# A low-rank layer's norm begun in the attention before it, its gates in two unequal parts, and its outputs in six PSUM banks

## The chip, the cores and the metric

The kernel runs on one core of a Trainium2 chip. The time is device microseconds of one launch, median of 3 runs. One profiled execution goes with it; all rows come from that one.

## What is computed

Eight layers are applied in turn to `x`, 16 batches of 128 rows of 128 numbers, all float32. The change touches the last two: a causal cross-attention with 16 heads, and a low-rank layer with softmax gates. Cut to them, the reference is:

```python
x = x + _L3_xattn_ref(_layernorm(x, axis=-1), ctx_1024, ctx_1024, ...)
x = x + _L3_ffn_ref(_layernorm(x, axis=-1), weight, gate_w, lora_U, lora_V)
return x

def _L3_ffn_ref(x, weight, gate_w, lora_U, lora_V):
    scaling = 1.0 / lora_U.shape[1]                       # 1/16
    xt = x.reshape(-1, D_in)
    gate = jax.nn.softmax(xt @ gate_w.T, axis=-1)         # 8 gates a row
    base = xt @ weight.T
    t = jnp.einsum('nh,erh->ner', xt, lora_U)             # 8 x 16 low-rank numbers
    lora = jnp.einsum('ne,eor,ner->no', gate, lora_V, t)
    return (base + scaling * lora).reshape(B, S, -1)
```

## The kernel before, in words

**Order.** `build` calls eight layer functions one after the other. Each opens a `Block` in which every engine has its own program; engines meet only at semaphores, and all of them at the barrier between two blocks. The sequence in each engine's program is written out by hand. `x` stays in SBUF as 16 batches of 128x128, and `xnT` is the normalised and transposed copy that the matmuls read.

**The attention** (`cross_attention`, tag `l3`, `causal=True`, keys made ahead). Every engine runs a software pipeline over `b` from 0 to B + 4 = 20. In iteration `b`, TensorE makes scores of batch `b` for the row maxima and of batch `b - 2` for the exponentials, weighs the values of batch `b - 3` (`weigh`, L503), turns the result (`turn`, L511), transposes it back (`flip_back`, L531) and multiplies by the output weight for batch `b - 4` (`project_out`, L536). ScalarE makes exponentials (L609) and moves results (L614, L618). GpSimd zeroes what lies past the diagonal (L430), once for each half of a batch; `weigh` waits for both halves. VectorE takes maxima, normalises (L688, L690), adds to `x` (L696), and takes the row statistics of batch `b - 5` (L126, L129). From `b` = 16 on there are no more maxima: the pipeline drains. Three PSUM banks form a ring (`Banks`) whose users take turns in a fixed order. After its 32 diagonal steps GpSimd computes the reciprocal standard deviation of batches 0 to 11 by a power (`scale_known`; L134, L137). TensorE ends with 12 transposes of the identity that nothing reads (L222), and the barrier follows.

**The low-rank layer** (`gated_lora`, tag `l3f`). It has three stretches.

- The norm (`RowNorm`). GpSimd makes the last four reciprocals, VectorE normalises 13 batches (L186) and ScalarE 3 (L200), TensorE transposes each (L195) into two banks `turn_ps`, and ScalarE copies four at a time to `xnT` (L211).
- The projections and gates. TensorE projects each batch to 128 low-rank numbers and 8 logits (L2256), into `both_ps`, which has six banks of three batches each; two unused slots repeat the last batch. VectorE takes maxima of the logits and subtracts (L2335, L2337), ScalarE makes exponentials (L2309), VectorE sums, inverts and forms the gates (L2342 to L2344). This is done in two halves of nine slots, `HALF = CHUNKS // 2 = 3` banks each.
- The chunks. There are six chunks `k`, of three batches, the last of one. VectorE multiplies the low-rank numbers by the gates (`lower`, L2349), TensorE transposes the product into the same bank of `both_ps` (`flip`, L2272), ScalarE copies it out (L2313), and TensorE adds two matmuls in one bank of `turn_ps`, `base` (L2267) and `widen` (L2278). VectorE adds that bank to `x` (`add`, L2355), and SyncE stores the chunk (L2248). Since there are two such banks, `base(k + 1)` waits for `add(k - 1)`: `pe.wait_ge(added, k - 1)` in `base`.

Of the kernel before, what the change touches and what calls it, by code (L numbers as in the profile page):

```python
# [15 lines left out]
P = 128  # L16
# [278 lines left out]
def cross_attention(nc, m, w, tag, meanwhile, masked_keys=False, causal=False, arrived=None, load_x=None, keys=None):  # L295
# [4 lines left out]
    with cleared_semaphores(nc, m) as new_semaphore, ExitStack() as ctx:  # L300
# [97 lines left out]
        def _(pool):  # L398
# [26 lines left out]
            if causal:  # L425
                for c in range(B):
                    for half in range(2):
# [3 lines left out]
                                                channel_multiplier=-1).then_inc(past_kept, 1)  # L431
            row_stats.scale_known(pool)

        @block.tensor
        def _(pe):
# [78 lines left out]
            def flip_late(i):  # L514
# [38 lines left out]
            for b in range(B + 5):  # L553
# [28 lines left out]
        def _(act):  # L582
# [55 lines left out]
            for b in range(B + 5):  # L638
# [14 lines left out]
                if exists(b - 2):  # L653
                    exponentials(b - 2, 1)
                if arrived is not None and b in LATE_GROUPS:
                    store_late_flips(LATE_GROUPS[b])
# [4 lines left out]
        def _(dve):  # L661
# [44 lines left out]
            for b in range(B + 5):  # L706
# [21 lines left out]
                if exists(b - 5):  # L728
                    dve.wait_ge(added, b - 4)
                    row_stats.take(dve, b - 5, b - 4)  # L730


# [1471 lines left out]
def gated_lora(nc, m, w, tag, meanwhile):  # L2204
# [3 lines left out]
    CHUNKS, BOTH = -(-B // PER), P + E  # L2208
    HALF = CHUNKS // 2
    x, xnT, identity = m["x"], m["xnT"], m["identity"]  # L2210
    with cleared_semaphores(nc, m) as new_semaphore, ExitStack() as ctx:  # L2211
# [3 lines left out]
        def ps(name, shape):  # L2215
# [12 lines left out]
            [new_semaphore(f"{tag}_{n}") for n in ("low_made", "flipped", "flip_stored", "out_made", "added", "stored")]  # L2228
        norm = RowNorm(nc, m, new_semaphore, tag, sb("xn", [P, B, D]), [turn_ps[i % 2][:, :, :] for i in range(NCH)],
                       sb("away", [P, B]))  # L2230
        block = ctx.enter_context(nc.Block())

        def batches(k):
            return range(PER * k, min(PER * k + PER, B))

        def held(t, k):
# [3 lines left out]
        def _(pool):  # L2240
            norm.pool(pool)

# [9 lines left out]
        def _(pe):  # L2252
            mm = nc.tensor.matmul

            def project(slot):
                ins = mm(both[:, slot // PER, slot % PER, :], xnT[:, min(slot, B - 1), :], w["down_gate"][:, :],  # L2256
                         start=True, stop=True)
                if slot + 1 in (HALF * PER, CHUNKS * PER):
                    ins.then_inc(both_made, 1)

            def base(k):
                if k < 2:
                    norm.wait_stored(pe, NCH - 2 + k)
                else:
                    pe.wait_ge(added, k - 1)
                for q, b in enumerate(batches(k)):
                    mm(turn_ps[k % 2][:, q, :], xnT[:, b, :], w["weight"][:, :], start=(q == 0), stop=False)  # L2267

# [6 lines left out]
            def widen(k):  # L2275
                pe.wait_ge(flip_stored, k + 1)
                for q, b in enumerate(batches(k)):
                    ins = mm(turn_ps[k % 2][:, q, :], low_t[:, b, :], w["up"][:, :], start=False,  # L2278
                             stop=(b == batches(k)[-1]))
# [12 lines left out]
            base(0)  # L2292
            base(1)
            flip(0)
            for k in range(CHUNKS):
                if k + 1 < CHUNKS:
                    flip(k + 1)
                    if k:
                        base(k + 1)
                widen(k)  # L2300

        @block.scalar
        def _(act):
            for i in range(NCH):
                norm.act(act, i)
            for h in range(2):
                part = slice(h * HALF * PER, (h + 1) * HALF * PER)
                act.wait_ge(below_made, h + 1)
                nc.scalar.activation(exps[:, part, :], below[:, part, :], ACT.Exp).then_inc(exps_made, 1)  # L2309
# [7 lines left out]
        def _(dve):  # L2317
            V = nc.vector
            chain = Chain(dve, step, 0)

            def part(h):
                return slice(h * HALF * PER, (h + 1) * HALF * PER)

            def logits(h):
                return both[:, h * HALF:(h + 1) * HALF, :, P:BOTH]

# [3 lines left out]
            def each_gate(row, h):  # L2330
                return row[:, part(h)].unsqueeze(2).broadcast_to([P, HALF * PER, E])

# [20 lines left out]
            def add(k):  # L2353
                dve.wait_ge(out_made, k + 1)
                V.tensor_tensor(held(x, k), held(x, k), turn_ps[k % 2][:, 0:len(batches(k)), :], ALU.add).then_inc(added, 1)  # L2355
# [8 lines left out]
            share(1)  # L2364
# [1076 lines left out]
```

## Time and profile before

| what | us |
|---|---|
| median of 3 runs | 1135.13 |
| lowest and highest of them | 1132.43, 1139.12 |
| the profiled execution | 1128.47 |
| its span, first to last instruction | 1126.7 |
| the low-rank layer, from its first instruction to its last addition | 1103.64 to 1123.73 |
| TensorE busy, share of the span | 954.4 (85%) |
| VectorE busy, share of the span | 755.2 (67%) |

The profiled execution is 6.7 us below the median of the runs. The page's totals are over eight layers with different limits; the change is in the last 50 us, so the rows below come from there. A row of the timeline merges neighbouring instructions of one line: its start, its length, and their count. A float32 matmul stands there as two records and a float32 transpose as one, so that x6 of L2267 is three batches and x3 of L2272 is three batches too.

### The profile page before, as it was taken

To read this page: it belongs to the slowest core of one execution; us is meant where nothing else is said; L and a number is where in the kernel's file an instruction comes from. 1 tells how busy PE (TensorE), PEld (TensorE's weight loads), DVE (VectorE), ACT (ScalarE), POOL (GpSimd) and SP (SyncE) were. 2 spreads that over 40 slices of the span, in tenths; PEclk is the share of its full clock that TensorE was granted. 3 is DMA by queue.
4 is the path that set the end of the run, shared out by engine and by line. 5 is a ranking of instruction groups with operands and counts; after the bars stand their busy time and mean duration, and the time that the engine had idled before them with its cause. 6 is when DMAs were issued, how large, how long until landed. Compare 5 with 4: busy or idle time off the path is not lost. (4 is left out here: it accounts for less than half of the span.)

```text
span 1126.7 us, 27897 instructions
## 1 busy us (share of the span) xinstructions
PE 954.4 (85%) x11407; PEld 663.6 (59%) x11407; DVE 755.2 (67%) x2039; ACT 581.4 (52%) x960; POOL 419.7 (37%) x438
## 2 busy tenths in 40 slices
PE   8998899999999988988898785776658586689997
PEld 6677445444544456777677483445446465557776
DVE  5886877557565555654575134688999999546764
ACT  4655565555555545634563551575554654335442
POOL 5310300000000024657002656356787978533341
PEclk9999999999999999999999897998878898799999
DMA  7000000000000025000000322000000000000001
GB/s 282 2 2 3 20 1 1 1 0 1 1 1 0 1 117 195 2 3 3 2 3 6 101 81 100 1 1 1 2 2 3 2 3 2 2 1 2 3 2 39
DMA packets 16301, 28.01 MB, mean 25 GB/s; under 512 B 1200, under 2 KB 13616, under 8 KB 15664
## 3 DMA queue, kind: packets, MB, share of 16 engines
q1 hardware_dynamic: 14864, 23.61, 5.9%
q0 software_dynamic: 1024, 2.10, 0.6%
q8 instruction: 92, 1.51, 0.6%
q10 hardware_dynamic: 288, 0.52, 0.2%
q14 instruction: 33, 0.27, 0.1%
HBM read 20.33 MB, written 5.90 MB: 23 GB/s over the span
## 5 line engine op out<-in xcount | busy, mean ns | idle before, releaser
L1490 PE MATMUL l0f_ctl<-l1f_in,l0f_in 128*128 128x512 f32 x320 | 143.9, 592 | 0.0
L134 POOL TENSOR_SCALAR row_var_eps<-row_mean_var 128x4 f32<-128x4 f32 (+1 forms) x20 | 4.5, 225 | 355.8 <-DVE row_mean_var L129 355.0
L669 DVE TENSOR_REDUCE l_neg_max<-l_ring 128x4 f32<-128x512 f32 x128 | 82.0, 682 | 43.4 <-PE l_ring L476 43.1
L609 ACT ACTIVATE l_probs<-l_scores 128x1024 f32<-128x1024 f32 x64 | 65.5, 1023 | 79.8 <-PE l_scores L484 79.8
L2938 ACT COPY l2f_blocks_sb<-l2f_right_t_sb 32x1024 f32<-32x1024 f32 x64 | 66.8, 1044 | 67.6 <-PE l2f_given_ps L2863 34.9
L1490 PEld LDWEIGHTS l0f_ctl<-l1f_in,l0f_in 128*128 128x128 f32 x320 | 60.9, 190 | 68.4 <-issue 66.3
L2863 PE MATMUL l2f_given_ps<-l2f_blocks_sb,l2f_left_t_sb 128*32 128x128 f32 x1024 | 47.7, 363 | 32.0 <-ACT l1f_in L2944 20.4
L833 POOL TENSOR_TENSOR l_squares<-l_exps 128x1024 f32<-128x1024 f32 x32 | 61.8, 1932 | 33.8 <-ACT l_exps L1103 33.8
L1196 DVE TENSOR_REDUCE l_neg_max<-l_scores 128x8 f32<-128x1024 f32 x32 | 39.2, 1225 | 43.2 <-PE l_scores L885 43.2
L2863 PEld LDWEIGHTS l2f_given_ps<-l2f_blocks_sb,l2f_left_t_sb 128*32 128x32 f32 x1024 | 41.9, 148 | 44.1 <-issue 43.9
L430 POOL TENSOR_SCALAR_AFFINE_SELECT l_probs<-l_probs 128x1024 f32<-128x1024 f32 x32 | 34.9, 1092 | 61.6 <-ACT l_probs L609 61.6
L1813 DVE TENSOR_SCALAR l0f_halt<-l0f_halt 128x512 f32<-128x512 f32 x8 | 3.4, 428 | 68.2 <-ACT l0f_halt L1695 68.2
L3018 POOL TENSOR_TENSOR l2f_factors_sb<-l2f_factors_sb,l1f_in 128x512 f32<-128x512 f32 x32 | 47.9, 1498 | 0.0
L1103 ACT ACTIVATE l_exps<-l_scores 128x1024 f32<-128x1024 f32 x32 | 32.8, 1024 | 28.7 <-PE l_scores L891 28.5
L1806 DVE SCALAR_TENSOR_TENSOR l1f_in<-l0f_index,l0f_in,l0f_hidden 128x512 f32<-128x512 bf16 x64 | 43.5, 747 | 4.3 <-ACT l0f_index L1674 3.6
L885 PE MATMUL l_scores<-l_k_heads,l_q_all 32*128 32x256 f32 x256 | 37.2, 407 | 8.7 <-DVE l_neg_max L1196 6.3
L1141 ACT ACTIVATE l_exps<-l_scores 128x1024 f32<-128x1024 f32 x32 | 31.0, 1021 | 19.8 <-PE l_scores L974 19.8
L2839 PE MATMUL l2f_sim_ps<-l1f_in,xnT 128*128 128x512 f32 x32 | 18.9, 675 | 26.0 <-DVE l1f_in L3047 25.8
L476 PE MATMUL l_ring<-l_k_heads,l_q_all 32*128 32x256 f32 x256 | 36.2, 399 | 4.4 <-ACT l_probs L609 2.9
L891 PE MATMUL l_scores<-l_q_all,l_k_heads 32*128 32x128 f32 x512 | 38.0, 288 | 1.8 <-ACT l_exps L1103 1.8
L484 PE MATMUL l_scores<-l_q_all,l_k_heads 32*128 32x128 f32 x512 | 37.1, 283 | 0.8 <-ACT l_probs L609 0.8
L484 PE MATMUL l_scores<-l_q_all,last_keys 32*128 32x128 f32 x512 | 37.1, 283 | 0.8 <-ACT l_probs L609 0.8
(499 smaller groups left out, 2703.3 us busy)
## 6 DMA issues: line engine op xcount, KB each, us to landing
l1f_in<-in_l1f SPq DMA_DIRECT2D x1, 4580.0 KB, 14.6
l0f_in<-in_l0f SPq DMA_DIRECT2D x1, 2304.0 KB, 8.4
l0f_in<-in_l2f SPq DMA_DIRECT2D x1, 2080.5 KB, 20.2
l1f_in<-in_l2u SPq DMA_DIRECT2D x1, 2048.0 KB, 9.3
sorted_rows<-first_in SPq DMA_DIRECT2D x1, 1856.0 KB, 11.5
l1f_sorted<-sorted_rows SPq DMA_DIRECT2D x7, 256.0 KB, 4.6
expert_rows<-l1f_sorted SPq DMA_DIRECT2D x7, 256.0 KB, 2.2
l_in<-in_l SPq DMA_DIRECT2D x1, 962.5 KB, 12.5
```

The costliest lines, as they stand in the source:

```text
L484: ins2 = mm(scores2[:, g, j, t, :], k_heads[r, c, t, j, :], q_all[r, c, t, :], start=True, stop=True, skip_group_check=True)
L609: nc.scalar.activation(probs[c % 2][:, 2 * pair:2 * pair + 2], scores2[:, :, :, :, :], ACT.Exp, scale=SCORE_SCALE).then_inc(exp_done, 1)
L669: ring.free(V.tensor_reduce(out, score_bank(b, half, g), AX.X, ALU.max, negate=True), ("score", b, half, g))
L833: nc.gpsimd.tensor_tensor(squares[c % 2][:, pair], e, e, ALU.mult).then_inc(squared, 1)
L885: ins1 = mm(scores1[:, g, :, t, :], q_all[r, b, t, :], k_heads[r, b, t, :, :], start=True, stop=True, skip_group_check=True)
L891: ins2 = mm(scores2[:, g, j, t, :], k_heads[r, c, t, j, :], q_all[r, c, t, :], start=True, stop=True, skip_group_check=True)
L1196: V.tensor_reduce(out, scores1[:, :, :, :, :].rearrange("p g j t s -> p (g j) t s"), AX.X, ALU.max, negate=True).then_inc(max_taken, 1)
L1490: return nc.tensor.matmul(out, lhs, rhs, start=start, stop=stop)
L1806: ins = STT(chosen[c % 2][:, k, p, :], index[k][:, c % 2, :], w["row_expert"][:, p:p + 1], hidden[c % 2][:, p, :], ALU.is_equal, ALU.mult)
L2863: ins = mm(given_ps[K * j:K * j + K, s, :, :], left_t[b % 2][:, 8 * j + s, :], blocks[:, 8 * j + s, :, :], start=True, stop=True)
L2938: A.copy(blocks[rows, :, u, :], right_t[rows, :, :]).then_inc(blocks_made, 1)
L3018: TT(value, value, kept[:, side, :, :], ALU.mult).then_inc(cut_made, 1)
```

## The change

In the attention, only where keys were made ahead (`l3`):

- After the diagonal steps of batch 12, GpSimd waits until eight batches have statistics and makes their reciprocals; after its last diagonal step it makes those of batches 8 to 11 alone.
- VectorE normalises batches 0 to 3 at the end of iteration 16 and batches 4 to 7 at the end of iteration 17 (`hand_on`), into `q_all`, whose queries are used up.
- TensorE transposes them in iterations 17 and 18 (`flip_handed`), between `turn` and `project_out`, into the ring; ScalarE copies them to `xnT` (`store_handed`).

In the low-rank layer:

- `RowNorm` goes. GpSimd makes the last four reciprocals at once, VectorE normalises batches 8 to 15, and TensorE transposes these into the last two banks of `both_ps`. ScalarE normalises nothing.
- TensorE projects batches 0 to 7 first, then `base(0)`, the transposes of 8 to 11, `base(1)`, the projections of 8 to 11, the transposes of 12 to 15, and the last six slots.
- The two parts of the gates are chunks 0 and 1 (six slots) and chunks 2 to 5 (twelve slots).
- The outputs of chunks 2 to 5 go into banks 0 to 3 of `both_ps`, each free once the copy L2313 of chunk `k - 2` is done. `base(k + 2)` stands behind `widen(k)`, and no matmul waits for an addition.
- `add(k - 2)` follows `lower(k)` on VectorE, before it was `add(k - 3)`.

The core of the diff:

```diff
@@ cross_attention
+        HANDED = {B: 0, B + 1: 1} if keys is not None else {}
+        if HANDED:
+            handed_rstd, handed_xn = sem("handed_rstd"), sem("handed_xn")
+        uses += [("handed", i) for i in HANDED.values()]
@@ gpsimd
+                    if HANDED and c == B - 4:
+                        pool.wait_ge(row_stats.combined, 8)
+                        row_stats.scale(pool, 0, 8).then_inc(handed_rstd, 1)
-            row_stats.scale_known(pool)
+            if HANDED:
+                pool.wait_ge(row_stats.combined, RowStats.KNOWN)
+                row_stats.scale(pool, 8, RowStats.KNOWN, step=2)
+            else:
+                row_stats.scale_known(pool)
@@ tensor
+            def flip_handed(i):
+                ring.wait_free(pe, ("handed", i), 0)
+                pe.wait_ge(handed_xn, 4 * i + 4)
+                for b in range(4 * i, 4 * i + 4):
+                    ins = nc.tensor.transpose(ring.bank(("handed", i))[:, b % 4, :], q_all[:, b, 0, :], identity[:, :])
+                ring.fill(ins, ("handed", i))
                 if exists(b - 3):
                     turn(b - 3)
+                if b - 1 in HANDED:
+                    flip_handed(HANDED[b - 1])
                 if exists(b - 4):
                     project_out(b - 4)
@@ scalar
+            def store_handed(i):
+                ring.wait_filled(act, ("handed", i), 0)
+                ring.free(nc.scalar.copy(xnT[:, 4 * i:4 * i + 4, :], ring.bank(("handed", i))[:, :, :]), ("handed", i))
@@ vector
+            def hand_on(i):
+                dve.wait_ge(handed_rstd, 1)
+                dve.wait_ge(scored2, 2 * (4 * i + 4))
+                for b in range(4 * i, 4 * i + 4):
+                    V.tensor_scalar(q_all[:, b, 0, :], x[:, b, :], m["row_mean_var"][:, b, 0:1], m["row_rstd"][:, b:b + 1],
+                                    ALU.subtract, ALU.mult).then_inc(handed_xn, 1)
@@ gated_lora
-    HALF = CHUNKS // 2
+    FIRST, HANDED = 2, 2
+        norm_bank = {i: both_ps[:, CHUNKS - NCH + i, :].rearrange("p (q s) -> p q s", q=4) for i in range(HANDED, NCH)}
+        def out_bank(k):
+            return turn_ps[k][:, :, :] if k < 2 else both_ps[:, k - 2, :].rearrange("p (q s) -> p q s", q=4)
@@ gpsimd
-            norm.pool(pool)
+            row_stats.scale(pool, RowStats.KNOWN, B).then_inc(rstd_made, 1)
+            clear_last_layers_semaphores(nc, m)
@@ tensor
             def base(k):
-                if k < 2:
-                    norm.wait_stored(pe, NCH - 2 + k)
-                else:
-                    pe.wait_ge(added, k - 1)
+                if k >= 2:
+                    pe.wait_ge(flip_stored, k - 1)
-            norm.pe(pe, 0)
-            norm.pe(pe, 1)
-            for i in range(NCH):
-                norm.wait_stored(pe, i)
-                for b in range(4 * i, 4 * i + 4):
-                    project(b)
-                if i + 2 < NCH:
-                    norm.pe(pe, i + 2)
-            for slot in range(B, CHUNKS * PER):
+            for b in range(4 * HANDED):
+                project(b)
+            base(0)
+            flip_norm(2)
+            base(1)
+            pe.wait_ge(xnT_stored, 1)
+            for b in range(8, 12):
+                project(b)
+            flip_norm(3)
+            pe.wait_ge(xnT_stored, 2)
+            for slot in range(12, CHUNKS * PER):
                 project(slot)
-            base(0)
-            base(1)
             flip(0)
             for k in range(CHUNKS):
                 if k + 1 < CHUNKS:
                     flip(k + 1)
-                    if k:
-                        base(k + 1)
                 widen(k)
+                if k + 2 < CHUNKS:
+                    base(k + 2)
@@ scalar
+            store_norm(2)
+            exponentials(0)
+            store_norm(3)
             for k in range(CHUNKS):
+                if k == 1:
+                    exponentials(1)
                 act.wait_ge(flipped, k + 1)
@@ vector
-            norm.dve(dve)
+            normalise(2)
             shift_down(0)
+            dve.wait_ge(rstd_made, 1)
+            normalise(3)
             share(0)
-            lower(0)
+            for k in range(FIRST):
+                lower(k)
             shift_down(1)
-            for k in range(1, HALF):
-                lower(k)
             share(1)
-            for k in range(HALF, CHUNKS):
+            for k in range(FIRST, CHUNKS):
                 lower(k)
-                add(k - HALF)
-            for k in range(CHUNKS - HALF, CHUNKS):
+                add(k - FIRST)
+            for k in range(CHUNKS - FIRST, CHUNKS):
                 add(k)
```

## Rows read from the trace of the kernel before

**Rows 1.** The chain that ended last, low-rank layer: start us, us, what.

```profile
1105.89 1.19 PE l3f_both_ps L2256 x8
1108.89 2.33 PE l3f_both_ps L2256 x20
...
1117.29 0.94 PE l3f_turn_ps L2267 x6
1118.22 0.68 PE l3f_turn_ps L2278 x6
1118.91 0.02 issue
1118.93 0.56 DVE x_in L2355
...
1122.98 0.55 DVE x_in L2355
```

**Rows 2.** Busy us of each engine by stretch, then PEclk, DMA share, GB/s.

```profile
1103.64:1112.29 8.65, 8.12 (x64) 7.35 (x65) 6.05 (x23) 4.03 (x9) 1.81 (x4) 1.00 0.00 1
1112.29:1123.73 11.44, 9.15 (x71) 7.77 (x69) 5.17 (x13) 2.56 (x6) 0.00 (x0) 1.00 0.19 70
1123.73:1126.70 2.97, 0.00 (x0) 0.00 (x0) 0.01 (x1) 0.00 (x0) 0.00 (x0) 1.00 0.26 88
680.00:690.00 10.00, 5.48 (x29) 4.63 (x30) 4.83 (x22) 0.58 (x1) 6.42 (x8) 0.68 0.23 73
```

**Rows 3.** Timeline, low-rank layer: start us, us, engine, line, what, [idle before <-releaser].

```profile
1103.66 3.42 DVE L186 TENSOR_SCALAR l3f_xn<-x_in,row_mean_var,row_rstd 128x128 f32<-128x128 f32 x13 [0.40 <-PEq L300]
...
1104.66 1.04 POOL L137 TENSOR_TENSOR row_rstd<-row_var_eps,first_in 128x4 f32<-128x4 f32 x1
...
1108.18 0.47 PEld L195 LDWEIGHTS l3f_turn_ps<-first_in,l3f_xn 128*128 128x128 f32 x4
...
1108.62 2.40 PEld L2256 LDWEIGHTS l3f_both_ps<-l3f_in,xnT 128*128 128x128 f32 x20
...
1108.93 0.58 ACT L211 COPY xnT<-l3f_turn_ps 128x512 f32<-128x512 f32 x1 [0.78 <-PE l3f_turn_ps L195]
...
1109.70 0.26 ACT L2309 ACTIVATE l3f_exps<-l3f_below 128x72 f32<-128x72 f32 x1 [0.18 <-DVE l3f_below L2337]
1109.99 0.23 DVE L2342 TENSOR_REDUCE l3f_total<-l3f_exps 128x9 f32<-128x72 f32 x1 [0.33 <-ACT l3f_exps L2309]
...
1110.77 0.56 DVE L2349 TENSOR_TENSOR l3f_low_rank<-l3f_both_ps,l3f_gates 128x384 f32<-128x384 f32 x1
1110.94 1.42 PEld L2267 LDWEIGHTS l3f_turn_ps<-l3f_in,xnT 128*128 128x128 f32 x12
...
1112.29 0.69 PEld L2272 LDWEIGHTS l3f_both_ps<-first_in,l3f_low_rank 128*128 128x128 f32 x6
...
1114.75 0.48 ACT L2313 COPY l3f_low_t<-l3f_both_ps 128x384 f32<-128x384 f32 x1 [0.97 <-PE l3f_both_ps L2272]
```

**Rows 4.** Waits in the chunks, 1112 to 1127: us in total, times, longest.

```profile
DVE x_in L2355 <- PE l3f_turn_ps L2278: 6.2, 5, 1.7
PEld l3f_turn_ps L2267 <- DVE x_in L2355: 2.4, 4, 0.8
```

**Rows 5.** Timeline of the attention's drain, columns as in rows 3.

```profile
1084.52 1.09 POOL L430 TENSOR_SCALAR_AFFINE_SELECT l_probs<-l_probs 128x1024 f32<-128x1024 f32 x1 [1.34 <-ACT l_probs L609]
...
1087.46 1.09 POOL L430 TENSOR_SCALAR_AFFINE_SELECT l_probs<-l_probs 128x1024 f32<-128x1024 f32 x1 [1.85 <-ACT l_probs L609]
...
1096.37 0.29 DVE L682 TENSOR_TENSOR l_v<-l_side_ps,l_in 128x128 f32<-128x128 f32 x1 [3.33 <-PE l_side_ps L527]
...
1098.19 1.08 PE L503 MATMUL l_o_ps<-l_probs,l_v 128*32 128x128 f32 x32 [1.42 <-POOL l_probs L430]
...
1098.51 2.29 POOL L137 TENSOR_TENSOR row_rstd<-row_var_eps,first_in 128x12 f32<-128x12 f32 x1
...
1099.34 0.37 ACT L614 COPY l_o<-l_o_ps 128x256 f32<-128x256 f32 x1 [2.36 <-PE l_o_ps L503]
...
1100.24 0.26 DVE L688 RECIPROCAL l_recip<-l_o_ps 128x16 f32<-128x16 f32 x1 [2.45 <-PE l_o_ps L511]
...
1101.24 0.27 ACT L618 COPY l_o_flat<-l_o_ps 128x128 f32<-128x128 f32 x1 [1.36 <-PE l_o_ps L531]
```

**Rows 6.** DMA issues of the output, 1119 to 1127: count, KB each, median us to landing.

```profile
out_x<-x_in SPq DMA_DIRECT2D x3, 192.0 KB, 2.0
out_x<-x_in SPq DMA_DIRECT2D x1, 64.0 KB, 1.8
```

More of the change, by code:

```diff
@@ L654, in _ @@
                     exponentials(b - 2, 1)
+                if b - 1 in HANDED:
+                    store_handed(HANDED[b - 1])
                 if arrived is not None and b in LATE_GROUPS:
@@ L730, in _ @@
                     row_stats.take(dve, b - 5, b - 4)
+                if b in HANDED:
+                    hand_on(HANDED[b])
 def tempered_attention(nc, m, w, tag, meanwhile):
@@ L2228, in gated_lora @@
             [new_semaphore(f"{tag}_{n}") for n in ("low_made", "flipped", "flip_stored", "out_made", "added", "stored")]
-        norm = RowNorm(nc, m, new_semaphore, tag, sb("xn", [P, B, D]), [turn_ps[i % 2][:, :, :] for i in range(NCH)],
-                       sb("away", [P, B]))
+        xn, row_stats = sb("xn", [P, B, D]), RowStats(nc, m, new_semaphore, tag + "_norm")
+        rstd_made, xn_made, xn_flipped, xnT_stored = \
+            [new_semaphore(f"{tag}_{n}") for n in ("rstd_made", "xn_made", "xn_flipped", "xnT_stored")]
+        norm_bank = {i: both_ps[:, CHUNKS - NCH + i, :].rearrange("p (q s) -> p q s", q=4) for i in range(HANDED, NCH)}
         block = ctx.enter_context(nc.Block())
@@ L2234, in batches, with chunks, part @@
             return range(PER * k, min(PER * k + PER, B))
+        def out_bank(k):
+            return turn_ps[k][:, :, :] if k < 2 else both_ps[:, k - 2, :].rearrange("p (q s) -> p q s", q=4)
+        def chunks(h):
+            return (slice(0, FIRST), slice(FIRST, CHUNKS))[h]
+        def part(h):
+            return slice(PER * chunks(h).start, PER * chunks(h).stop)
         def held(t, k):
@@ L2257, in project @@
                          start=True, stop=True)
-                if slot + 1 in (HALF * PER, CHUNKS * PER):
+                if slot + 1 in (FIRST * PER, CHUNKS * PER):
                     ins.then_inc(both_made, 1)
             def base(k):
-                if k < 2:
-                    norm.wait_stored(pe, NCH - 2 + k)
-                else:
-                    pe.wait_ge(added, k - 1)
+                if k >= 2:
+                    pe.wait_ge(flip_stored, k - 1)
                 for q, b in enumerate(batches(k)):
-                    mm(turn_ps[k % 2][:, q, :], xnT[:, b, :], w["weight"][:, :], start=(q == 0), stop=False)
+                    mm(out_bank(k)[:, q, :], xnT[:, b, :], w["weight"][:, :], start=(q == 0), stop=False)
             def flip(k):
@@ L2297, in _, with store_norm, exponentials @@
                     flip(k + 1)
-                    if k:
-                        base(k + 1)
                 widen(k)
+                if k + 2 < CHUNKS:
+                    base(k + 2)
         @block.scalar
         def _(act):
[L2304 to L2307, printed above, removed]
+            def store_norm(i):
+                act.wait_ge(xn_flipped, i - HANDED + 1)
+                nc.scalar.copy(xnT[:, 4 * i:4 * i + 4, :], norm_bank[i]).then_inc(xnT_stored, 1)
+            def exponentials(h):
                 act.wait_ge(below_made, h + 1)
-                nc.scalar.activation(exps[:, part, :], below[:, part, :], ACT.Exp).then_inc(exps_made, 1)
+                nc.scalar.activation(exps[:, part(h), :], below[:, part(h), :], ACT.Exp).then_inc(exps_made, 1)
+            store_norm(2)
+            exponentials(0)
+            store_norm(3)
             for k in range(CHUNKS):
+                if k == 1:
+                    exponentials(1)
                 act.wait_ge(flipped, k + 1)
@@ L2319, in _ @@
             chain = Chain(dve, step, 0)
-            def part(h):
-                return slice(h * HALF * PER, (h + 1) * HALF * PER)
             def logits(h):
-                return both[:, h * HALF:(h + 1) * HALF, :, P:BOTH]
+                return both[:, chunks(h), :, P:BOTH]
             def by_chunk(a):
@@ L2330, in each_gate @@
             def each_gate(row, h):
-                return row[:, part(h)].unsqueeze(2).broadcast_to([P, HALF * PER, E])
+                return row[:, part(h)].unsqueeze(2).broadcast_to([P, part(h).stop - part(h).start, E])
             def shift_down(h):
@@ L2354, in add, with normalise @@
                 dve.wait_ge(out_made, k + 1)
-                V.tensor_tensor(held(x, k), held(x, k), turn_ps[k % 2][:, 0:len(batches(k)), :], ALU.add).then_inc(added, 1)
-            norm.dve(dve)
+                V.tensor_tensor(held(x, k), held(x, k), out_bank(k)[:, 0:len(batches(k)), :], ALU.add).then_inc(added, 1)
+            def normalise(i):
+                for b in range(4 * i, 4 * i + 4):
+                    V.tensor_scalar(xn[:, b, :], x[:, b, :], m["row_mean_var"][:, b, 0:1], m["row_rstd"][:, b:b + 1],
+                                    ALU.subtract, ALU.mult).then_inc(xn_made, 1)
+            normalise(2)
             shift_down(0)
+            dve.wait_ge(rstd_made, 1)
+            normalise(3)
             share(0)
-            lower(0)
+            for k in range(FIRST):
+                lower(k)
             shift_down(1)
-            for k in range(1, HALF):
+            share(1)
+            for k in range(FIRST, CHUNKS):
                 lower(k)
-            share(1)
-            for k in range(HALF, CHUNKS):
-                lower(k)
-                add(k - HALF)
-            for k in range(CHUNKS - HALF, CHUNKS):
+                add(k - FIRST)
+            for k in range(CHUNKS - FIRST, CHUNKS):
                 add(k)
```

6 lines of the change are left out of this document (5 added, 1 removed).

## The prediction

> **What bounds the kernel now.** I read the chain that ended last first, because the change is at the end of the program, where every microsecond saved on the chain is a microsecond of the time. In the low-rank layer the chain runs on TensorE, with ScalarE and VectorE only between its pieces [rows 1]. The busy table splits the layer in two. Up to 1112.29, where the first `flip` starts, TensorE is busy 8.12 of 8.65 us; in the chunks after that 9.15 of 11.44 us [rows 2]. So the first stretch is bound by TensorE's own work, and the second has holes. The waits name them: four waits of `base` (L2267) for an addition, 2.4 us at the weight load [rows 4]. The chain shows the loop behind them: `base` 0.94, `widen` 0.68, the addition 0.56, then `base` again, 1117.29 to 1119.54, hence 2.25 us a chunk [rows 1]. The last addition ends at 1123.73, that is 20.09 us after the layer's start at 1103.64, and 2.97 us of storing follow [rows 2].
>
> The attention's drain is the opposite. VectorE idles 3.33 us and 2.45 us, ScalarE 2.36 and 1.36, TensorE 1.42 [rows 5]. Work put there may cost nothing.
>
> **Unit prices.** I take them from starts of consecutive weight loads, since the busy lengths overlap. Four transposes of the norm go from 1108.18 to 1108.62: 0.44, or 0.11 each. Twenty records of L2256, from 1108.62 to their end at 1111.22 (the chain's 1108.89 + 2.33), take 2.60 us; the next weight load starts at 1110.94, so ten slots issue in 2.32, 0.233 a slot, and their result is there 0.28 later. `base` for six batches issues in 1.35 (1110.94 to 1112.29), 0.67 a chunk, and `widen` the same by the chain's 0.68. `flip` of three batches is 0.34. A stored copy of four batches is 0.58 on ScalarE, one of three 0.48; exponentials 0.26; VectorE normalises a batch in 0.263 (3.42 / 13); the small gate operations come 0.26 apart and `lower` is 0.56 [rows 1, 3]. A hand-over between engines is 0.02 to 0.04.
>
> **The change in the drain.** Added to GpSimd behind the diagonal steps of batch 12: a power over 8 columns. It isn't in the trace; 4 columns take 1.04 and 12 take 2.29 [rows 3, 5], hence about 1.67, and 1.95 with the addition before it; bounds 1.3 and 2.6. The next diagonal step starts at 1084.52 after 1.34 of idle, so it slips by 0.6 (bounds 0 to 1.3). `weigh` needs the second half of that batch too, whose step starts at 1087.46 after 1.85 of idle: the slip is swallowed there. Cost nought; without that cover it would be 0.6.
>
> Added to VectorE: twice four normalisations, 1.05 us each. The first lie in the 3.33 idle before 1096.37, the second in the 2.45 before 1100.24. Nought. Added to ScalarE: two copies of 0.58. The first is in the 2.36 before 1099.34. The second ends at about 1101.29, and the copy L618 behind it would have started at 1101.24: 0.05. Added to TensorE: twice 0.44. The first falls in the 1.42 before 1098.19. The second stands ahead of `project_out(14)` and delays it by 0.44; behind that stands `flip_back(15)`, which waits for VectorE until 1100.87 and starts as before, as it needs TensorE from about 1100.65. What is late then is the copy L618 by 0.05, and with it the last `project_out`, addition and statistics. I take 0.05 for the drain, bounds 0 and 0.5 (the whole of one group of transposes). GpSimd's last power shrinks from 12 columns to 4 and gains nothing, because GpSimd waits at the barrier anyway.
>
> **The change in the layer.** I write the new order out, t counted from the layer's first instruction. TensorE starts at once, as eight batches lie in `xnT`: slots 0 to 7 until 1.92, `base(0)` until 2.59, four transposes until 3.03 (results 3.30). VectorE has normalised 8 to 11 by 1.15, so nobody waits for it. ScalarE copies until 3.90; TensorE, with `base(1)` in between until 3.70, waits 0.24 and projects 8 to 11 until 4.87. Four transposes until 5.31 (results 5.58), ScalarE's copy until 6.18: TensorE waits 0.91. The last six slots run until 7.62, their results at 7.89.
>
> Meanwhile the first gates: logits at 1.72, but the exponentials stand behind the first copy on ScalarE and end at 4.1; VectorE's three operations until 4.9, `lower(0)` and `lower(1)` until 5.96. Both are made before `flip(0)` can start at 7.62, so the first part's gates, on the chain before, are hidden entirely. `flip(0)` and `flip(1)` issue until 8.28, ScalarE copies until 8.72, `widen(0)` and `base(2)` run from 8.76 to 10.10 (a wait of 0.48).
>
> The second part now has twelve slots. VectorE shifts from 7.91 to 8.43, the exponentials follow ScalarE's first copy, 8.72 to 8.95, three operations until 9.75, `lower(2)` until 10.33. `flip(2)` starts at 10.38: a wait of 0.27. From there TensorE never stops: `flip(2)`, `widen(1)`, `base(3)`, `flip(3)`, `widen(2)`, `base(4)`, `flip(4)`, `widen(3)` are three times 0.34 and five times 0.67, to 14.75; a third of `base` and of `flip` for chunk 5 adds 0.33; `widen(4)` gives its result 0.94 later, at 16.02. The addition ends at 16.60, that of one batch behind it at 16.80. In the steady part a chunk costs TensorE 0.34 + 0.67 + 0.67 = 1.68 us where it cost 2.25. VectorE has 0.56 + 0.56 for it and is no bound.
>
> **Sum.** 20.09 - 16.80 = 3.3 us in the layer, less 0.05 in the drain: 3.2. By places, about 2.3 us are the waits for additions, and the rest is what the eight handed transposes and the hidden gates leave after the new waits of 0.24, 0.91, 0.48 and 0.27. The stores keep their tail: the last two additions come as close together as before, and the one before them lies 1 us ahead while 192 KB land in about 2.0 [rows 6]; I allow up to 0.3 for that.
>
> The profiled execution of 1128.47 would become 1125.3. The median of the runs lies 6.7 us above it, and I carry the saving over unchanged: 1135.13 - 3.2 = 1131.9.
>
> **Rivals.**
>
> *TensorE never waits (a larger gain).* Its issue work in the layer after the change is 18 slots of 0.233, 16 batches of `base` and `widen` at 0.224 each, and 24 transposes of 0.11, together 14.0 us; with the tail of 0.27 + 0.02 + 0.56 + 0.20 the layer can't be below 15.1, a gain of 5.0: 1130.1. For it: ScalarE and VectorE have slack. Against it: `flip_norm(3)`, its copy and the last six slots are strictly one behind the other.
>
> *The change does not do what it says (about no gain).* TensorE was busy 8.12 of 8.65 us in the first stretch, so handing on eight batches could free 0.88 us of its transposes there and bring back more in waits for copies, if those in the new order are half as long again as I have them; and if VectorE's additions fall behind (they now follow `lower(k)` with one chunk less between), part of the 2.3 us stays. I give this a gain of 0.5 to 1.5: 1134.1.
>
> *TensorE's clock falls (slower).* In this stretch the granted clock is 1.00, 2.4 GHz; in 680 to 690 us, with TensorE busy 5.48 of 10 us, it is 0.68, a mix of the two levels [rows 2]. If the new waits brought it to 1.2 GHz in the layer, each microsecond of TensorE's 14.0 us of issue work would become two: 3.2 us of work at the lower level eat the gain, and all of it makes the layer 14.0 - 3.2 = 10.8 us slower than before: 1145.9. Against it: even before, with 2.4 us of waits in the chunks, the clock stayed, and the new longest wait is 0.91. The Trainium skill says in "TensorE: Matmul & The Clock Gate", section "A second HAM failure mode: psum-queue depth-cycling", that a kernel which cycled its outputs through PSUM banks idled briefly between groups often enough for the clock to swing between its levels. Taken as a rule it speaks against this change, which cycles outputs through six banks instead of two; the trace, which shows 1.00 with two banks and longer idle, doesn't bear it out.
>
> **How the numbers follow.** My forecast, a gain of 2 to 4.5 us, has a chance of 0.73; the larger gain 0.09; no gain 0.13; the slower clock, or any other loss, 0.05. About 0.5% (5.7 us) is what a measurement of this kernel can tell from no change. Even the largest gain, 5.0 us, is below it, so "faster by over 0.5%" comes about only through the spread of the runs, which is 6.7 us between the lowest and the highest of three: I give it 0.17, slower 0.05, and the same 0.78. The range goes from the profiled execution's own result, 1125.3, to the highest run less the saving, 1139.12 - 3.2 = 1135.9; it leaves the slow clock out.
>
> **What would show it.** Right: L2267 has no wait for L2355 at all; additions of the last full chunks about 1.7 us apart where they were 2.25 apart; eight batches' transposes and copies in the drain with the barrier within 0.1 us of its place; about 16.8 us from the layer's first instruction to the last addition; the clock at 1.00. Wrong: waits of L2256 for the copy of `xnT` above 1 us; `flip(2)` waiting long for `lower(2)`; the diagonal step that starts at 1087.46 later than that; VectorE between chunks without idle. The prediction fails if a float32 matmul record no longer issues every 0.11 us, or if the runs' spread hides 3 us.

## The result and the profile after

The changed kernel takes 1126.46 us (median; 1120.32 to 1136.17), beside 1134.28 us for the kernel before in the same comparison. The ratio is 0.9946, with a 95% interval from 0.9923 to 0.9969: 6.1 us saved, between 3.5 and 8.7. (The plain quotient of the two medians is 0.9931, 7.8 us; the ratio, here and below, is estimated from all single runs and isn't that quotient.) Forecast were 3.2 us and a time of 1131.9, in a range from 1125.3 to 1135.9. The profiled execution took 1124.08 us, where 1125.3 was forecast.

The chain that ended last, in the changed kernel (start us, us, what); it answers to rows 1:

```profile
1102.38 2.09 PE l3f_both_ps L2303 x16
...
1107.92 0.59 ACT xnT L2357
...
1110.58 0.49 ACT l3f_low_t L2371
1111.07 0.04 issue
1111.11 0.94 PE l3f_turn_ps L2323 x6
1112.05 0.67 PE l3f_both_ps L2312 x6
1112.72 0.02 issue
1112.73 0.55 PE l3f_both_ps L2317 x3
...
1114.62 0.33 PE l3f_both_ps L2317 x3
1114.95 0.67 PE l3f_both_ps L2323 x6
1115.62 0.67 PE l3f_both_ps L2312 x6
...
1118.32 0.56 DVE x_in L2410
```

The addition (L2410, before L2355) stands only at the chain's end. Between 1112.73 and 1118.32 there is nothing but TensorE, and three pieces make a chunk: 0.33 + 0.67 + 0.67 = 1.67 us, where it was 2.25.

The busy table of the changed kernel, with the layer split at the first `flip` as in rows 2:

```profile
1102.34:1109.94 7.60, 6.88 (x56) 6.48 (x57) 4.18 (x15) 1.31 (x3) 1.20 (x2) 1.00 0.00 1
1109.94:1119.07 9.13, 8.31 (x71) 7.69 (x69) 5.82 (x15) 2.73 (x7) 0.00 (x0) 1.00 0.22 79
```

The first stretch went from 8.65 to 7.60 us, the second from 11.44 to 9.13: 3.36 us together (3.40 if the changed layer is counted from its first matmul at 1102.38 and not from 1102.34, as is done from here on). The granted clock is 1.00 in both. The waits of TensorE that are left, from the timeline of its weight loads:

```profile
1106.25 0.99 PEld L2303 LDWEIGHTS l3f_both_ps<-l3f_in,xnT 128*128 128x128 f32 x8 [0.20 <-ACT xnT L2357]
...
1108.56 1.46 PEld L2303 LDWEIGHTS l3f_both_ps<-l3f_in,xnT 128*128 128x128 f32 x12 [0.91 <-ACT xnT L2357]
...
1111.11 0.74 PEld L2323 LDWEIGHTS l3f_turn_ps<-l3f_in,l3f_low_t 128*128 128x128 f32 x6 [0.48 <-ACT l3f_low_t L2371]
...
1112.73 0.31 PEld L2317 LDWEIGHTS l3f_both_ps<-first_in,l3f_low_rank 128*128 128x128 f32 x3 [0.21 <-DVE l3f_low_rank L2404]
```

And the drain of the attention, timeline, answering to rows 5:

```profile
1082.27 1.66 POOL L137 TENSOR_TENSOR row_rstd<-row_var_eps,first_in 128x8 f32<-128x8 f32 x1
...
1083.89 1.11 POOL L434 TENSOR_SCALAR_AFFINE_SELECT l_probs<-l_probs 128x1024 f32<-128x1024 f32 x1
...
1086.18 1.09 POOL L434 TENSOR_SCALAR_AFFINE_SELECT l_probs<-l_probs 128x1024 f32<-128x1024 f32 x1 [1.18 <-ACT l_probs L633]
...
1095.08 0.29 DVE L708 TENSOR_TENSOR l_v<-l_side_ps,l_in 128x128 f32<-128x128 f32 x1 [2.12 <-PE l_side_ps L545]
...
1096.90 1.08 PE L514 MATMUL l_o_ps<-l_probs,l_v 128*32 128x128 f32 x32 [0.98 <-POOL l_probs L434]
...
1098.96 0.26 DVE L714 RECIPROCAL l_recip<-l_o_ps 128x16 f32<-128x16 f32 x1 [1.20 <-PE l_o_ps L522]
```

Every idle of rows 5 has shrunk by about the work put into it, or by the slip that it took up: VectorE 3.33 to 2.12 and 2.45 to 1.20, TensorE 1.42 to 0.98, GpSimd 1.85 to 1.18. From the last weighing to the layer's first instruction it is 5.48 us, before 5.45.

So 3.4 us are explained in the two layers that were changed. The two profiled executions differ by 4.7 us in span, and the runs by 6.1. The last attention's first scores come at 999.7 us in the profiled execution of before and at 998.4 in that of after, 1.3 us earlier, in code that the change doesn't touch. From there to the low-rank layer's first instruction it is 103.9 us before and 104.0 after, so the last attention, with all that was put into it, is as long as it was. The 4.7 us are thus 1.3 ahead of it and 3.4 in the low-rank layer. Whether the change does something ahead of it was the open question.

### The profile page after: what moved, and what is told of

The parts are those of the page before. It is cut to its first block and busy times, and to the rows that moved or that the text cites. A ratio compares the mean times of both kernels' runs of the same rounds, so it can differ in the third digit from the quotient of the medians.

```text
span 1122.0 us, 27901 instructions
## 1 busy us (share of the span) xinstructions
PE 951.4 (85%) x11407; PEld 659.3 (59%) x11407; DVE 756.3 (67%) x2042; ACT 580.0 (52%) x957; POOL 419.3 (37%) x438
## 5 line engine op out<-in xcount | busy, mean ns | idle before, releaser
L134 POOL TENSOR_SCALAR row_var_eps<-row_mean_var 128x4 f32<-128x4 f32 (+2 forms) x21 | 4.8, 229 | 361.4 <-DVE row_mean_var L129 356.5
L2924 PE MATMUL l2f_given_ps<-l2f_blocks_sb,l2f_left_t_sb 128*32 128x128 f32 x1024 | 44.8, 347 | 28.0 <-ACT l1f_in L3005 18.3
L2924 PEld LDWEIGHTS l2f_given_ps<-l2f_blocks_sb,l2f_left_t_sb 128*32 128x32 f32 x1024 | 39.4, 142 | 41.3 <-issue 41.0
L2900 PE MATMUL l2f_sim_ps<-l1f_in,xnT 128*128 128x512 f32 x32 | 20.5, 726 | 29.7 <-DVE l1f_in L3108 29.5
## 6 DMA issues: line engine op xcount, KB each, us to landing
sorted_rows<-first_in SPq DMA_DIRECT2D x1, 1856.0 KB, 11.5
```

The costliest lines, as they stand in the source:

```text
L2924: ins = mm(given_ps[K * j:K * j + K, s, :, :], left_t[b % 2][:, 8 * j + s, :], blocks[:, 8 * j + s, :, :], start=True, stop=True)
```

## The experiments

Two theories. **A**: the change saves 3.3 us, all in the low-rank layer, because its TensorE no longer waits for additions; what was measured beyond that is upstream spread. **B**: it also shortens something upstream by 2.8 us. Below, "the layer" is the time from its first instruction (where that is a weight load, from the matmul 0.03 us behind it) to the end of its last addition. It is read from one profiled execution of each kernel; three executions with the changed layer unaltered gave 16.69 us each time.

**The changed kernel once more**, and **a placebo**, that is the kernel before with an edit that should do nothing:

> The changed kernel once more, unaltered. Theory A: all that the change does lies in the low-rank layer, which takes 16.7 us instead of 20.1, so the true saving is 3.3 us, a ratio of 0.9971, and what was measured beyond that (6.1 us) comes from layers that the change doesn't touch, whose lengths vary from one execution to the next; here the ratio may come out anywhere around 0.997. Theory B: the change also shortens something upstream by some 2.8 us, and the ratio comes out at 0.9946 again. Both expect 16.7 us from the layer's first instruction to its last addition.

```diff
         row_stats = RowStats(nc, m, new_semaphore, tag)
+        if keys is not None:
+            unused = sem("unused_a"), sem("unused_b")
```

> The kernel before with two semaphores more in the last attention, which nobody waits for: the bookkeeping of the change without its work. Theory A: no difference, a ratio of 1.000 within the interval, and the low-rank layer at 20.1 us. Theory B, if the upstream part comes from the bookkeeping: 0.9975.

Measured: the changed kernel 1127.45 us beside 1132.33, ratio 0.9974 (0.9945 to 1.0004), layer 16.69; the placebo 1131.59, ratio 1.0011 (0.9979 to 1.0043), layer 20.10. The second comparison of the changed kernel lands on A's 0.9971 and not on B's 0.9946, though its interval holds both. More telling is where the spread sits. The weight loads of the last attention's first scores (their line, shapes and count, min/median/max ns, first and last start us), in three executions: of the changed kernel once more, of the placebo, and of the run with equal parts below.

```profile
L487 PEld LDWEIGHTS l_ring<-last_keys,l_q_all x256: 181/184/185, 999.0 to 1084.9; 32*128 32x128 f32 x128
```

```profile
L478 PEld LDWEIGHTS l_ring<-last_keys,l_q_all x256: 181/185/185, 1002.6 to 1088.6; 32*128 32x128 f32 x128
```

```profile
L487 PEld LDWEIGHTS l_ring<-last_keys,l_q_all x256: 181/184/185, 1011.0 to 1096.9; 32*128 32x128 f32 x128
```

In the changed kernel's first execution the start was 998.4. All three run the same instructions up to there, and begin at 999.0, 1002.6 and 1011.0; from there these weight loads take 85.9 or 86.0 us in each. The placebo's delay of 3.6 us against the first of them is older: an earlier attention's score loads (tile `l_k_heads`) already run from 425.8 to 515.9 us there, and from 422.3 to 512.3 in the other, and from there to the last attention both take 486.7 us. The kernel with equal parts is at 513.4 at that point, so nearly all its delay comes behind it. The stretch from 600 to 1000 us in the changed kernel (its first execution) and in the one with equal parts (columns as in rows 2):

```profile
600.00:1000.00 400.00, 281.35 (x4124) 221.03 (x4124) 291.57 (x965) 205.39 (x398) 258.28 (x278) 0.88 0.07 22
```

```profile
600.00:1000.00 400.00, 285.31 (x4056) 229.88 (x4057) 284.33 (x936) 199.97 (x385) 251.60 (x264) 0.84 0.07 22
```

The granted clock is 0.88 in one and 0.84 in the other, and the slower one has done less by 1000 us (4056 matmuls against 4124). In single runs the whole time goes with the run's mean granted clock: about 0.85 us for each 0.001 in the kernel before (0.77 to 1.00 in the other sets of runs). A straight line of time over clock, read at a clock of 0.950, gives 1130.6 for before (35 runs of the second comparison; the clocks of the first one's weren't kept), 1130.9 for the placebo, and 1127.0 and 1126.9 for the changed kernel in its two comparisons: 3.6 and 3.7 us, near the layer's 3.4. That is a reckoning and has no interval of its own, but it agrees with A, and nothing agrees with B except the first ratio. Lines through their own runs give 1128.2 for the six banks alone and 1127.0 for the transposes ahead (both below): 2.4 and 3.6 us, where their layers are 2.5 and 3.5 shorter.

**The six banks alone**, on the kernel before:

```diff
-                    pe.wait_ge(added, k - 1)
+                    pe.wait_ge(flip_stored, k - 1)
                 for q, b in enumerate(batches(k)):
-                    mm(turn_ps[k % 2][:, q, :], xnT[:, b, :], w["weight"][:, :], start=(q == 0), stop=False)
+                    mm(out_bank(k)[:, q, :], xnT[:, b, :], w["weight"][:, :], start=(q == 0), stop=False)
...
                     flip(k + 1)
-                    if k:
-                        base(k + 1)
                 widen(k)
+                if k + 2 < CHUNKS:
+                    base(k + 2)
```

> The kernel before with nothing but the outputs of chunks 2 to 5 in the projections' banks, and the base of chunk k + 2 behind the widening of chunk k. Theory A: the norm stretch stays at 8.65 us until the first transpose, the chunks go at 1.68 us instead of 2.25, and the last addition ends 17.6 us after the layer's start, a gain of 2.5 us of the 3.3. A rival, that the waits for additions only move to the gates of the second half, gives 19 to 20 us. Ratio by theory A 0.998.

Measured: layer 17.55, the first transpose of a chunk (its weight load) 8.65 us after the layer's start in both kernels; ratio 0.9978 (0.9951 to 1.0005). Not shown in the diff are the same replacement of the bank in `widen` and `add`. So 2.5 of the 3.4 us come from this one edit. It holds two things, more banks and a base that moved from ahead of `widen(k)` to behind it; no run has the banks with the old order, so how much of the 2.5 us the order gives isn't shown.

**The handing alone** (two banks, parts of nine slots), and **the changed kernel with two banks**. The second one's edit is the reverse of the diff above; the first has `FIRST = 3` in addition.

> The changed kernel with two output banks again and the gates in two parts of nine slots: only the norm of eight batches is handed on. If the waits for additions bound the chunks, what is won in the norm is lost again: the first addition ends at about 11.8 us after the layer's start (before: 11.35), since the normalisation of the last four batches now stands behind the first part's maxima on VectorE; then 2.25 us a chunk, and the last addition at 20.5 us. A rival, that each part of the change gives a share of its own, expects 19 us or less. In the attention's drain both expect no change (5.5 us from the last weighing to the layer's first instruction).

> The changed kernel with two output banks again (base waits for an addition), but with the unequal parts and the handing. First addition at 10.8 us, then 2.25 us a chunk: the last at 19.5 us, if the banks carry most of the gain. If handing and parts carry it, 18 us or less.

Measured: 20.24 and 19.51. The handing alone is 0.15 us slower than the kernel before in this layer, although it took eight transposes out. Waits of the handing alone in the chunks (engine line <- waited for: us, times, longest):

```profile
DVE x_in L2410 <- PE l3f_turn_ps L2323: 5.7, 4, 1.7
PEld l3f_turn_ps L2312 <- DVE x_in L2410: 2.9, 4, 1.0
```

The loop of additions and bases is intact, and its waits are 2.9 us instead of 2.4 [rows 4]. The first addition sets when the loop starts, and it starts 10.94 us after the layer does, before 10.79. From there to the end all three kernels with two banks take 9.30 us: the changed kernel with two banks, whose first addition starts at 10.21, ends at 19.51. So nothing is lost inside the loop; all that counts is when its first addition comes.

With the handing alone TensorE is ahead: the first widening is issued 9.54 us after the layer's start, before 9.81. What is late is VectorE, which has another piece in its queue ahead of the first addition, with no idle between them:

```profile
1113.06 0.56 DVE L2404 TENSOR_TENSOR l3f_low_rank<-l3f_both_ps,l3f_gates 128x384 f32<-128x384 f32 x1
1113.54 0.54 DVE L2410 TENSOR_TENSOR x_in<-x_in,l3f_turn_ps 128x384 f32<-128x384 f32 x1
```

In the kernel before VectorE waited 0.50 us for the widening at that point. The expectation had the first addition end at 11.8 us; it ended at 11.5.

**The changed kernel with equal parts**, and **banks and parts without the handing**:

```diff
-    FIRST, HANDED = 2, 2
+    FIRST, HANDED = 3, 2
```

> The changed kernel with the gates in two parts of nine slots, six banks and the handing. The first part's logits are there only after slot 8, so its maxima come ahead of the last normalisations on VectorE at 4.6 us, these end at 6.2, and the last six projections at 8.6 instead of 7.6. The wait of 0.2 for the third chunk's gates vanishes. Last addition at 17.5 us, against 16.7 with unequal parts. If the parts don't matter, 16.7.

> The kernel before with six output banks and the unequal parts, and the whole norm in the layer. The norm stretch is 8.65 us again; the second part's exponentials now stand behind the first copy, so the third transpose waits 0.2 us for its gates: last addition at 17.8 us, 1.0 us more than the changed kernel. If handing is worth nothing, 16.7; if it is worth all of its moved work (8 transposes, two copies, 8 normalisations), above 19.

Measured: 17.27 and 17.78. Why the parts matter shows in the timeline of VectorE with equal parts:

```profile
1119.37 0.23 DVE L2390 TENSOR_REDUCE l3f_neg_top<-l3f_both_ps 128x9 f32<-128x72 f32 x1 [3.29 <-PE l3f_both_ps L2303]
1119.64 0.23 DVE L2392 TENSOR_TENSOR l3f_below<-l3f_both_ps,l3f_neg_top 128x72 f32<-128x72 f32 x1
1119.79 1.11 DVE L2414 TENSOR_SCALAR l3f_xn<-x_in,row_mean_var,row_rstd 128x128 f32<-128x128 f32 x4
```

The maxima of the first part wait 3.29 us for slot 8, and the last four normalisations stand behind them, until 1120.90, 5.9 us after the layer's start. In the changed kernel they wait 0.55 us, and the normalisations are done at 3.1. The layer in seven of the eight combinations (two banks with unequal parts and no handing wasn't run):

| banks | parts | handing | layer, us | expected |
|---|---|---|---|---|
| 2 | 9 + 9 | no (before) | 20.09 | |
| 2 | 9 + 9 | yes | 20.24 | 20.5 |
| 2 | 6 + 12 | yes | 19.51 | 19.5 |
| 6 | 9 + 9 | no | 17.55 | 17.6 |
| 6 | 6 + 12 | no | 17.78 | 17.8 |
| 6 | 9 + 9 | yes | 17.27 | 17.5 |
| 6 | 6 + 12 | yes (after) | 16.69 | 16.8 |

The parts of the change aren't additive. Handing brings 0.28 us with equal parts and 1.09 with unequal ones (six banks both times). Unequal parts cost 0.23 us without the handing, where the third transpose waits 0.2 us for its gates as expected, and bring 0.58 with it. The banks bring 2.54 us on the kernel before and 2.82 (19.51 - 16.69) on top of the other two.

**Two more powers on GpSimd**, to see what hid the first one:

```diff
                         row_stats.scale(pool, 0, 8).then_inc(handed_rstd, 1)
+                        for h in (slice(0, 8), slice(8, 16)):
+                            nc.gpsimd.tensor_tensor(norm.away[:, h], m["row_var_eps"][:, 0:8], m["minus_half"][:, 0:8], ALU.pow)
```

> The changed kernel with two more powers over eight columns on GpSimd, whose results nobody reads, behind the one that the change put after the diagonal steps of batch 12. In the changed kernel the power shifts the next diagonal step by 0.7 us and nothing later. Each further power takes 1.66 us: the first diagonal step of batch 13 ends about 3.4 us later, and the second, which the weighing waits for, starts 2.2 us later. If the slack on GpSimd is what hid the power (my reading), the time from the first of these small operations to the low-rank layer's first instruction grows from 20.4 to 22.4 us. If GpSimd is off the path altogether, it stays at 20.4.

Measured, in its timeline:

```profile
1085.58 0.21 POOL L134 TENSOR_SCALAR row_var_eps<-row_mean_var 128x8 f32<-128x8 f32 x1
1085.87 1.66 POOL L137 TENSOR_TENSOR row_rstd<-row_var_eps,first_in 128x8 f32<-128x8 f32 x1
1087.50 3.25 POOL L440 TENSOR_TENSOR l_away<-row_var_eps,first_in 128x8 f32<-128x8 f32 x2
1090.70 3.19 POOL L434 TENSOR_SCALAR_AFFINE_SELECT l_probs<-l_probs 128x1024 f32<-128x1024 f32 x3
```

Three diagonal steps now run without a gap. The layer starts at 1107.93, 22.35 us after 1085.58; in the changed kernel it is 20.40 (1081.98 to 1102.38). Of the 3.25 us that were added, 1.95 reach the end; the slack that the changed kernel had left there is 1.18, which would let 2.07 through. The power of the change is free because of this slack, and what goes beyond it is paid nearly in full. The low-rank layer itself is 16.69 us again.

**The transposes of the first chunks ahead of the last projections**, an attempt to fill the waits of 0.91 and 0.48:

```diff
             flip_norm(3)
+            flip(0)
+            flip(1)
             pe.wait_ge(xnT_stored, 2)
             for slot in range(12, CHUNKS * PER):
                 project(slot)
-            flip(0)
             for k in range(CHUNKS):
-                if k + 1 < CHUNKS:
+                if k and k + 1 < CHUNKS:
                     flip(k + 1)
...
-                if k == 1:
+                if k == 2:
                     exponentials(1)
```

> The changed kernel with the transposes of chunks 0 and 1 ahead of the last six projections, and the exponentials of the second part behind the second copy. Their input is ready at 5.3 and 5.8 us after the layer's start, while TensorE waits from 5.3 to 6.2 for the copy of xnT. If the layer is bound by TensorE's order and its waits (my reading), 0.67 us of work moves into that wait, and the waits of 0.48 (first widening for its copy) and 0.21 (third transpose for its gates) vanish: 16.7 - 1.36 = 15.4 us. If it is bound by VectorE or by the stores, it stays at 16.7. Against the kernel before, theory A gives a ratio of 0.9959 (4.7 us), theory B 0.9934.

Measured: layer 16.57, a gain of 0.12 where 1.36 was expected; ratio 0.9972 (0.9945 to 0.9999). The transposes did move into the wait, but a new one opened, in the timeline of weight loads:

```profile
1115.14 0.75 PEld L2323 LDWEIGHTS l3f_turn_ps<-l3f_in,l3f_low_t 128*128 128x128 f32 x6
1115.81 0.75 PEld L2312 LDWEIGHTS l3f_both_ps<-l3f_in,xnT 128*128 128x128 f32 x6
1117.80 0.31 PEld L2317 LDWEIGHTS l3f_both_ps<-first_in,l3f_low_rank 128*128 128x128 f32 x3 [1.24 <-DVE l3f_low_rank L2405]
1118.08 0.75 PEld L2323 LDWEIGHTS l3f_turn_ps<-l3f_in,l3f_low_t 128*128 128x128 f32 x6
```

My expectation had filled the time of the second part's gates with work that is ready by then, and overlooked that it stands in the queue behind the instruction that waits. `widen(1)` (1118.08) and the base behind it, 1.34 us, could have run during those 1.24 us.

**The same with that work ahead of the wait:**

```diff
-            for k in range(CHUNKS):
-                if k and k + 1 < CHUNKS:
+            for k in range(2):
+                widen(k)
+                base(k + 2)
+            flip(2)
+            for k in range(2, CHUNKS):
+                if k + 1 < CHUNKS:
                     flip(k + 1)
                 widen(k)
                 if k + 2 < CHUNKS:
                     base(k + 2)
```

On VectorE the order becomes `lower(2)`, `lower(3)`, `add(0)`, `add(1)`, `lower(4)`, `add(2)`, `lower(5)`, and the remaining additions.

> The transposes of chunks 0 and 1 ahead of the last six projections as in the run with the flips first, and now also both widenings of the first part and the bases of chunks 2 and 3 ahead of the third transpose; on VectorE the gates' products of chunks 2 and 3 come ahead of the first two additions. The run with the flips first left TensorE idle for 1.24 us ahead of the third transpose, with 1.34 us of ready work (second widening, fourth base) queued behind it. If that order was what held the gain back, the third transpose starts at 10.2 us with no wait above 0.1, the fifth to last pieces run without a hole from 11.4 us, and the last addition ends at 15.8 us after the layer's start (flips first: 16.57, changed kernel: 16.69). If something else bounds it (VectorE's second gates, the copies), 16.3 or more. Ratio to the kernel before by the layer alone: 4.3 of 1132 us, 0.9962.

Measured: layer 15.81. The chain of this kernel:

```profile
1109.81 0.67 PE l3f_turn_ps L2323 x6
1110.48 0.67 PE l3f_both_ps L2312 x6
1111.15 0.67 PE l3f_turn_ps L2323 x6
1111.82 0.67 PE l3f_both_ps L2312 x6
1112.49 0.34 PE l3f_both_ps L2317 x3
1112.83 0.02 issue
1112.85 0.49 ACT l3f_low_t L2376
```

The wait for the gates is gone; a wait of 0.41 us for one copy is left. By the layer this version beats both kernels, 4.28 us below before and 0.88 below the changed one, as expected to 0.01. Two orders changed at once, TensorE's and VectorE's, and no run tells their shares apart. By the times of the runs it can't be told from the changed kernel: it takes 1130.28 us beside 1132.25 for the kernel before, ratio 0.9975 (0.9948 to 1.0003), where the changed kernel had 0.9946 and 0.9974; single executions go from 1122.69 to 1134.68. At a clock of 0.950 the straight lines give 1126.0 for it and 1130.0 for before.

## Why the prediction was right, and where it was off

**What bounds the kernel.** Right: the chunks were held by `base` waiting for an addition. Taking that wait away, with the base moved behind the widening and nothing else, gave 2.5 us.

**The drain.** Right. The power over 8 columns took 1.66 us (1.67 taken), the diagonal step behind it started at 1083.89 without idle, and the next one still had 1.18 us to spare. From the last weighing on the drain grew by 0.03 us, 0.05 taken. The added powers show that this cover was real and finite.

**The layer.** Every wait came out where it was put: 0.20, 0.91, 0.48 and 0.21 us for 0.24, 0.91, 0.48 and 0.27. A chunk takes 1.67 us for 1.68, the layer 16.69 for 16.80. Half of these 0.11 us are a slip of the prediction's first term: eight slots of 0.233 are 1.86 us (1.81 in the trace), where it wrote 1.92, and everything behind stands later by that. The saving in the profile's layer is 3.4 us for 3.3. The tail from the last addition to the end is 2.93 us, before 2.97: the closer stores cost nothing that shows.

**By places.** Right in size: I put 2.3 us to the waits for additions and left 1 us to handing and gates together, and the banks alone gave 2.5 and the rest 0.9. Wrong as a sum of independent shares: with two banks and equal parts the handing costs 0.15 us, because VectorE reaches the first addition later, and with six banks three quarters of its 1.09 us hang on the unequal parts.

**The carry-over to the median.** This is where the size was off. I took 1135.13 - 3.2 = 1131.9; the median was 1126.46, the ratio 0.9946 for the 0.9972 that 3.2 us make, just outside the interval's upper end of 0.9969. The 6.1 us lie above the forecast of 2 to 4.5, and above the 5.0 that the layer could give if TensorE never waited; only the layer's own 3.4 us fall inside it. That 1126.46 lies in the stated range is luck: the lower end, 1125.3, came from a profiled execution that happened to be 6.7 us below its median. "Faster by over 0.5%", as that comparison has it, had 0.17, for just this reason, the spread of the runs; in the second comparison the ratio was 0.9974, within 0.5%, and its interval reaches 1.0004, so that there the spread does hide 3 us, as the prediction's last line feared. The unchanged instructions ahead of the last attention took anything from 998.0 to 1011.0 us in the profiled executions here. That the 2.8 us above the layer's saving are this spread is argued from the repeat, the placebo and the clocks. It isn't shown beyond doubt, as the intervals are 0.5% wide.

**The rivals.** "TensorE never waits" gave 15.1 us as the floor of the layer; the best order tried came to 15.81. "No gain" was wrong for the whole, though it is what the handing does with two banks and equal parts. The clock stayed at 1.00 with the outputs going through six banks. By the trace TensorE was busy 8.31 of 9.13 us in the chunks, a larger share than the 9.15 of 11.44 before; its longest wait there was 0.48 us, and 0.91 in the layer. So the swinging clock that the Trainium skill describes in "TensorE: Matmul & The Clock Gate", section "A second HAM failure mode: psum-queue depth-cycling", for a kernel that cycled through PSUM banks didn't come to pass here.

## What to carry to other kernels

On an engine that works its queue in order, write out the order with start and end of each piece before moving anything: an independent instruction behind a waiting one isn't filler, as the attempt with 0.12 us instead of 1.36 shows, and moving the ready work ahead of the wait, on TensorE and VectorE together, brought 0.76 more. Take the loop-carried wait first (a buffer that comes free only through another engine's last step); while it stands, work removed ahead of it counts only if the loop's first release comes earlier (first additions at 10.94, 10.79 and 10.21 us gave layers of 20.24, 20.09 and 19.51). When a change is worth 0.3% and executions spread by 1.5%, judge it by the changed stage in the profile, and let a placebo and a repeat say what the whole time can show.

## What the runs showed of the hardware

Most of the spread of this kernel's time arises in the layers between 512 and 1000 us. From the last score load of an earlier attention (512.3 to 515.9 us in the profiled executions) to the first of the last attention it took from 484.4 us (changed kernel) to 497.6 (equal parts). From 600 to 1000 us TensorE is busy 70% or 71% of the time and its granted clock is a mix of the two levels, 0.84 to 0.88. Where TensorE is busy over 90% and the granted clock is 1.00, the length hardly varies: the last attention's score loads took 85.9 or 86.0 us in all profiled executions but one, and the low-rank layer of the changed kernel took 16.69 us three times. The exception is the kernel with the transposes first, with 88.7 us: there the granted clock was 0.66 from 1000 to 1010 us, and single score loads took 333 ns, where the longest of the last attention's in the others is 186. GpSimd's power takes 1.04 us for four columns, 1.66 for eight and 2.29 for twelve, that is 0.16 us for each column more.
